# Slot 0's gather ahead of the last x_new stores, expert 1's loads held for slot 1's rows

## The reference

```python
x = x + tanh(g_xattn) * matmul(fake_quant(layernorm(x)), fake_quant(ctx))      # ctx (2, 1024, 1024), 8-bit steps
x = x + tanh(g_ffn) * moe(layernorm(x))
# moe: logits = y @ W_gate + b_gate; the two best of 8 experts per token;
#      mean over the two of relu(y @ W_e[expert] + b_e[expert]),  W_e (8, 1024, 1024)
```

## Time and profile before

| | us |
|---|---|
| median of 3 runs | 361.48 |
| lowest and highest | 359.96, 361.72 |
| the profiled execution | 358.4 |
| its span in the trace | 356.6 |
| TensorE busy (matmuls) | 311.2 |
| VectorE busy | 242.3 |
| GpSimd busy | 170.7 |
| ScalarE busy | 152.0 |

### The profile page before, as it was taken

How to read it: one execution, slowest core, us unless ns; L and a number is a source line. 1 busy time by engine, 2 the same in 40 slices (tenths; PEclk the granted TensorE clock), 3 DMA queues, 4 the chain that set the end, 5 groups by cost and what they waited for, 6 DMA issues and landing times.

```text
span 356.6 us, 6660 instructions
## 1 busy us (share of the span) xinstructions
PE 311.2 (87%) x1590; PEld 237.5 (67%) x1599; DVE 242.3 (68%) x328; ACT 152.0 (43%) x167; POOL 170.7 (48%) x168
## 2 busy tenths in 40 slices
PE   4488989999743999999999979999999999999920
PEld 1133336879712687888878868888888888888810
DVE  3789999998750897589975955985339854954520
ACT  3868979855352191076713610811118114600100
POOL 5647610000044473674845755746547465757430
PEclk9999999996585999999999989999999999999985
DMA  6999913335876569679999996896558965646432
GB/s 226 414 409 388 376 78 119 141 156 180 348 201 274 209 233 391 136 172 377 340 419 266 286 348 143 205 413 187 115 118 214 404 156 145 134 78 140 76 78 45
DMA packets 19965, 81.47 MB, mean 228 GB/s; under 512 B 4208, under 2 KB 4208, under 8 KB 15856
## 3 DMA queue, kind: packets, MB, share of 16 engines
q1 hardware_dynamic: 12272, 57.71, 42.5%
q0 software_dynamic: 7536, 23.60, 28.2%
q10 hardware_dynamic: 144, 0.01, 0.0%
HBM read 62.43 MB, written 18.87 MB: 228 GB/s over the span
## 4 chain that ended last, share of the span: by engine, by line
PE 49%; DVE 17%; DMA 13%; issue 8%; ACT 6%; DVEq 3%; POOL 1%; ACTq 1%; SPq 0%; POOLq 0%
PE ps L1254 37%; DMA out_dram<-res,sidx 6%; DVE w_lo L859 3%; PE ps_y L1078 2%; PE ps L1051 2%; DMA y_rows<-y_scratch,idx 2%; ACT w_hi L673 2%; DVE st L721 2%; DMA stage<-in_L_ffn_W_e_dram 2%; DMA stage<-in_ctx_dram 2%; PE ps_s L1103 2%; DVEq L287 2%; PE ps_q L1103 2%; DVE xt L777 1%; DVE res L1013 1%
## 5 line engine op out<-in xcount | busy, mean ns | idle before, releaser
L473 POOL DMA_INDIRECT y_rows<-y_scratch,gidx x88 | 107.2, 1218 | 35.0 <-issue 25.9
L1254 PE MATMUL ps<-w_hi,yT_hi 128*128 x320 | 99.6, 393 | 3.5 <-DVE yT_lo L853 3.5
L1254 PE MATMUL ps<-w_lo,yT_hi 128*128 x320 | 99.2, 391 | 0.0
L1254 PE MATMUL ps<-w_hi,yT_lo 128*128 x320 | 99.0, 391 | 0.0
L1254 PEld LDWEIGHTS ps<-w_hi,yT_hi 128*128 128x128 f32 x320 | 60.1, 189 | 17.6 <-issue 5.4
L859 DVE TENSOR_TENSOR w_lo<-stage,w_hi 128x2048 f32 (+1 forms) x32 | 71.2, 2278 | 0.9 <-ACT w_hi L673 0.8
L1254 PEld LDWEIGHTS ps<-w_lo,yT_hi 128*128 128x128 f32 x320 | 60.6, 189 | 12.6
L1254 PEld LDWEIGHTS ps<-w_hi,yT_lo 128*128 128x128 f32 x320 | 60.4, 189 | 12.7
L644 ACT ACTIVATE yT_hi<-ps_y 128x1024 fp32r<-128x1024 f32 x21 | 21.5, 1023 | 106.4 <-PE ps L1254 74.8
L499 POOL DMA_INDIRECT out_dram<-res,sidx x20 | 32.3, 1616 | 66.6 <-DVE res L1015 44.1
L1013 DVE TENSOR_TENSOR res<-ps,bias 128x1024 f32<-128x1024 f32 x20 | 24.4, 1220 | 47.6 <-PE ps L1254 37.4
(11 more groups left out here) (163 smaller groups left out, 248.8 us busy)
## 6 DMA issues: line engine op xcount, KB each, us to landing
stage<-in_L_ffn_W_e_dram SPq DMA_DIRECT2D x32, 1024.0 KB, 7.4
stage<-in_ctx_dram SPq DMA_DIRECT2D x16, 512.0 KB, 11.2
xt<-in_x_dram SPq DMA_DIRECT2D x8, 512.0 KB, 11.1
y_scratch<-y SPq DMA_DIRECT2D x8, 512.0 KB, 3.4
bias<-in_L_ffn_b_e_dram SPq DMA_DIRECT2D x8, 512.0 KB, 4.8
out_dram<-xt SPq DMA_DIRECT2D x6, 512.0 KB, 5.7
y_rows<-y_scratch,gidx POOLq DMA_INDIRECT x88, 4.4
out_dram<-xt POOLq DMA_DIRECT2D x2, 512.0 KB
```

The source lines that it names most:

```text
L473: pool.indirect_dma_start(out=y_rows[q][:, b * QD:(b + 1) * QD], out_offset=None, in_=y_quarters[:, :], in_offset=bass.IndirectOffsetOnAxi ...
L1254: last = pe.matmul(ps[q][:, h * 512:(h + 1) * 512], lhs[q][:, k, :], w[:, bass.ds(woff + k * D + h * 512, 512)], start=(k == 0 and lhs is ...
```

## The change

- POOL: three small indirect gathers of row 0 of W_gate into a new tile `prime` come after its last centring; the stores of x_new 6 and 7 move from ahead of slot 0's gather to behind slot 2's.
- SyncE: expert 1's chunks 0 and 1 go ahead of y stores 4 to 7. After x_new 0 to 3 the queue waits for slot 0's rows, then come bias 0 and x_new 4 and 5; it waits for slot 1's rows, then come bias 1 and chunks 2 and 3.
- ScalarE: the adds for tiles 6 and 7 come after the evacuation of slot 0; the waits for the x_new stores move from ahead of the slot loop to `sidx` (tiles 6 and 7) and to the splits (tiles 0 to 5).
- VectorE: the row sums of batch row 0 are read after the second slot matrix; the low split of chunk 2 goes ahead of slot 0's `yT_lo`; the waits for the stores move to the result's step.
- TensorE: the row-sum products and the place-rows products change places with the second count, and 18 clock-keeping matmuls stand in one place instead of 2 and 14.

```diff
--- before.py
+++ after.py
@@ -144,6 +144,7 @@
         idx = sb("idx", [P, E * SPE], u32)
         weight = sb("weight", [P, E * SPE], f32)
         qidx = sb("qidx", [P, (E + 1) * SPE, NQ], u32)
+        prime = sb("prime", [P, 3, E], f32)
         gidx = sb("gidx", [P, 2, NQ], u32)
         sidx = sb("sidx", [P, 2], u32)
 
@@ -230,6 +231,7 @@
         s_free = sem("slot_psum_free")
         s_post = sem("slot_result_ready")
         s_sc = sem("slot_scattered")
+        s_prime = sem("queue_primed")
         s_settled = sem("waits_settled")
 
         block = ctx.enter_context(nc.Block())
@@ -339,15 +341,19 @@
                 load_w0(c)
             for i in range(TPB):
                 store_y(i)
+            load_w1(0)
+            load_w1(1)
             for i in range(TPB, NT):
                 store_y(i)
-            load_w1(0)
-            load_w1(1)
-            for i in range(NT - 2):
+            for i in range(TPB):
                 store_x_new(i)
+            sp.wait_ge(s_g[0], 16)
             sp.wait_ge(s_qt, NT)
-            for e in range(2):
-                load_bias(e)
+            load_bias(0)
+            for i in range(TPB, NT - 2):
+                store_x_new(i)
+            sp.wait_ge(s_g[1], 16 * NQ)
+            load_bias(1)
             load_w1(2)
             load_w1(3)
             with sp.Fori(2, E) as n:
@@ -463,9 +469,10 @@
             pool.iota(iota_pe[:, :, :], [[1, P], [0, E]], base=0, channel_multiplier=0,
                       allow_small_or_imprecise_dtypes=True).then_inc(s_iota, 1)
             centre_q1(6)
-            for i in (NT - 2, NT - 1):
-                pool.wait_ge(s_oa, i + 1)
-                pool.dma_start(out_t[i], xt[:, i, :]).then_inc(s_sc, 16)
+            for j in range(3):
+                pool.indirect_dma_start(out=prime[:, j, :], out_offset=None, in_=W_gate[:, :],
+                                        in_offset=bass.IndirectOffsetOnAxis(ap=qidx[:, E * SPE, 0:1], axis=0)
+                                        ).then_inc(s_prime, 16)
 
             def gather(q):
 
@@ -484,8 +491,12 @@
             pool.wait_ge(s_gi, 2)
             pool.wait_ge(s_perm, 2)
             gather(0)
+            for i in (NT - 2, NT - 1):
+                pool.wait_ge(s_oa, i + 1)
+                pool.dma_start(out_t[i], xt[:, i, :]).then_inc(s_sc, 16)
             pool.wait_ge(s_oi, 16 * (NT - 2))
             pool.wait_ge(s_sc, 32)
+            pool.wait_ge(s_prime, 48)
 
             def step(slot, q, turn):
                 pool.wait_ge(s_gi, slot * 2 + 3)
@@ -636,7 +647,7 @@
             keep_yT(6)
             normalise(7)
             keep_yT(7)
-            for i in range(NT):
+            for i in range(NT - 2):
                 add_rowsum(i)
 
             def evacuate_hi(slot, q):
@@ -660,9 +671,9 @@
                                ACT.Copy).then_inc(s_perm, 1)
             act.wait_ge(s_tp, 1)
             evacuate_hi(0, 0)
+            for i in (NT - 2, NT - 1):
+                add_rowsum(i)
             act.wait_ge(s_tab, 1)
-            act.wait_ge(s_oi, 16 * (NT - 2))
-            act.wait_ge(s_sc, 32)
 
             def step(slot, q, turn):
                 act.wait_ge(s_mm, slot + 1)
@@ -677,11 +688,13 @@
                 act.wait_ge(s_tp, slot + 2)
                 evacuate_hi(slot + 1, 1 - q)
                 pick_rows(slot + 3, 1 - q)
+                act.wait_ge(s_sc, 32)
                 act.wait_ge(s_sc, slot * 16 + 16)
                 settle(act)
                 col = entry(act, COL, slot, E * SPE - 1)
                 act.activation(sidx[:, q:q + 1], idx[:, bass.ds(col, 1)], ACT.Copy).then_inc(s_gi, 1)
                 with act.If(nxt > 0):
+                    act.wait_ge(s_oi, 16 * (NT - 2))
                     for c in range(NCH):
                         split_hi(c)
                 act.nop()
@@ -919,11 +932,11 @@
             make_onehot(3)
             select(1)
             sign(1)
-            read_rowsums(0)
             positions(1)
             make_onehot(4)
             make_onehot(5)
             slot_matrix(1)
+            read_rowsums(0)
             select(2)
             make_onehot(6)
             sign(2)
@@ -982,14 +995,12 @@
                 dve.transpose(ps_y[:, :, :].rearrange("p k (b r) -> p k b r", b=NQ),
                               y_rows[q][:, :].rearrange("p (b k r) -> p k b r", b=NQ, k=KT)).then_inc(s_tp, 1)
 
+            split_lo(2, 3, slice(2 * CW, 3 * CW))
             dve.wait_ge(s_eh, 1)
             evacuate_lo(0)
-            for c in range(NCH // 2, NCH):
-                split_lo(c, c + 1, slice(c * CW, (c + 1) * CW))
+            split_lo(3, 4, slice(3 * CW, 4 * CW))
             dve.wait_ge(s_el, 1)
             turn_rows(1, 1)
-            dve.wait_ge(s_oi, 16 * (NT - 2))
-            dve.wait_ge(s_sc, 32)
 
             def step(slot, q, turn):
                 nxt = entry(dve, NXT, slot, E - 1)
@@ -1009,6 +1020,7 @@
                         settle(dve)
                 col = entry(dve, COL, slot, E * SPE - 1)
                 dve.wait_ge(s_mm, slot + 2)
+                dve.wait_ge(s_sc, 32)
                 dve.wait_ge(s_sc, slot * 16 + 16)
                 dve.tensor_tensor(res[q][:, :], ps[q][:, :], bias[:, bass.ds(woff >> 3, D)], ALU.add).then_inc(s_free, 1)
                 dve.wait_ge(s_free, slot + 3)
@@ -1213,22 +1225,20 @@
             pe.wait_ge(s_xn, NT - 1)
             pe.matmul(ps_i.rearrange("p (a b) -> p a b", b=E), ones_b[:, :],
                       sel[:, NT:NT + 1, :].to_broadcast([P, SPE, E]), start=True, stop=False)
-            place_rows(0, 0, 2)
             transpose_y(7)
+            counts(1)
             rowsums(0)
-            counts(1)
             gate(7)
-            place_rows(0, 2, TPB)
+            place_rows(0, 0, TPB)
             counts(2)
             place_rows(1, TPB, NT - 1)
             place_rows(2, NT - 1, NT)
-            keep_clock(2, ps[0][:, 512:1024])
             pe.wait_ge(s_abs, 1)
             for b in range(NQ):
                 last = pe.matmul(ps_r[:, b * E * SPE:(b + 1) * E * SPE], spread[:, b, :], tok_abs[:, :], start=True, stop=True)
             last.then_inc(s_spread, 1)
             rowsums(1)
-            keep_clock(14, ps[0][:, 512:1024])
+            keep_clock(18, ps[0][:, 512:1024])
             for k in range(KT):
                 if k % (KT // 2) == 0:
                     pe.wait_ge(s_perm, 1 + k // (KT // 2))
```

## The result

The changed kernel takes 364.35 us (median of 4 runs, 362.63 to 365.95) against 360.72 for the kernel before (4 runs, 358.06 to 361.72). The ratio is 1.0126, 95% interval 1.0073 to 1.018: slower by 0.7 to 1.8%. The forecast was 358.5, so it had the wrong sign. The profiled execution took 364.41 us, with a span of 362.6.

The account below looks back on a forecast made before the run. Taken as bound: the chain through expert 1's weight splitting and scatters, then TensorE from 208.82 us. Split 3.4 us earlier, 0.6 clock loss, a tenth or two for indices: -3.0, 361.5 to 358.5 us; range 353.7 to 361.8.

Parts of the forecast that it names:

- The frame: TensorE's earlier start at slot 0 pays only as far as the splitting of expert 1's weights comes earlier too.
- Slot 0's first matmul: TensorE's start on slot 0: at 106.5 us, 11.4 us earlier, with ends of 106.0 and 113.0.
- GpSimd's gathers: Eight quarter gathers for slots 1 and 2: 10.0 us, plus 2.0 for stretching under VectorE's splits, ending at 113.1.
- The failed step: Landing of the x_new 6 and 7 stores, ahead of expert 1's split: near 120.5, bounds 117.5 and 124.6.
- Rival 2: No change: stores count as landed only when the whole backlog has moved, 122.1 to 123.5; some 361.0 us; chance 0.21.
- Rival 3: Slower: backlog at 297 GB/s or less, stores last, landing 125.5; +2.2 us, 363.7 us; chance 0.10.
- From landing to split: On ScalarE, from the x_new stores' landing to expert 1's first split: 1.2 us.
- S: How much earlier ScalarE starts expert 1's first split: 3.4 us, at 121.7 instead of 125.14.
- The clock: Half clock on TensorE after the idle gap before slot 2: 2.0 us lost, 1.4 hidden behind scatter 1, loss 0.6.
- The sum: Whole kernel: -3.4 + 0.6 = -2.8, and a tenth or two for earlier indices: -3.0 us.
- The second slow stretch: Slow clock behind TensorE's gap ending at 208.82: may vanish for up to 2.0 us gain; none taken.
- Early loads, small gathers: Expert 1's chunks 0 and 1: cost 0, 1 us at most; GpSimd's small gathers: nothing, bounds 0.1 gain, 0.5 loss.

Follow-up runs that it names:

- the repeat: The kernel before, unchanged, profiled a second time: 360.98 us, span 359.2, indices at 100.57 us; ratio 0.9973.
- e10: The changed kernel without SyncE's hold for slot 0's rows, the hold for slot 1's rows kept: ratio 1.0132.
- e6: The changed kernel without SyncE's two holds, for slot 0's and slot 1's rows: ratio 0.9884.
- e9: The changed kernel without SyncE's hold for slot 1's rows, the hold for slot 0's rows kept: ratio 0.9987.
- e5: The kernel before with only slot 0's gather moved ahead of the stores of x_new 6 and 7: ratio 0.9815.
- e12: The changed kernel without the three small gathers on GpSimd and their wait: ratio 1.0149.
- e7: The changed kernel without both SyncE holds and with the stores of x_new 6 and 7 ahead of slot 2's gathers: ratio 0.987.
- e3: The changed kernel with the stores of x_new 6 and 7 between slot 1's and slot 2's gathers: ratio 1.0008.

## Why the prediction was wrong

Times of the forecast are moved by the 3.66 us that lie between the two traces of the kernel before, so that they compare with the repeat.

- **The frame was right.** "a PE start that is x us earlier is worth x only if the splitting of expert 1 comes x us earlier too": TensorE's start came 9.8 us earlier, and the whole of it was lost. From split to slot 2 it is 15.3 us before, in the repeat and after (125.14 to 140.42, 128.76 to 144.10, 130.20 to 145.47).
- **Slot 0's first matmul**: 11.4 us earlier forecast, 9.8 measured. ScalarE takes up the rows when it was to (105.25; 105.4 forecast); the missing 1.6 us lie between there and the first matmul, and cost nothing at the end. Indices: 0.35 and 0.7. Slot 1's pick: 104.7 forecast, 104.49 measured.
- **GpSimd's gathers**: two were lengthened, to 2.93 and 2.00, 3.0 us of stretch where 2.0 was forecast. First store 117.1 forecast, 117.69 measured.
- **The failed step: "The stores, sharing from 115.2, land near 120.5."** That is 6.0 us from the second issue; it took 10.67. In the repeat's frame it is 124.2 forecast and 129.0 measured: 4.8 us. Three things were wrong in it. The stores got no equal share, but landed behind the whole backlog; by the prediction's own sum that ends at 122.1, 125.8 in this frame, 1.6 later than 124.2. The backlog moved more slowly: 4.2 MB were to take 11.1 us from 111 (114.7 here), and took about 13.2 from 113.8 to 127, some 317 GB/s, 1.2 later. And between the end of the bulk and the landing lie 2.0 us more, for which the prediction had no term. Together 4.8; even its outer bound, 124.6, is 128.3 here. Behind it all stands a cause that no rival named: I had counted the volume, but not that the holds leave the queues at 111 and 114 GB/s from 100 to 108 and at 166 from 112 to 116, so that everything comes at once. Rival 2 had the first of the three: its backlog is moved at 123.5 at the latest, 127.2 here, which is what the windows show, but without the last 2 us. Rival 3 had the first two, "297 GB/s or less" and "the stores last", and a landing at 125.5, or 129.2 here, right to 0.2 us. I gave it 0.10. Part of that hit is luck: the rate until 127 was above 297, and the 2.0 us made up for it.
- **From landing to split**: 1.2 forecast, 1.2 measured. So S is -1.4 instead of 3.4.
- **The clock**: 2.0 us of loss forecast, "of that, 1.4 hide". Measured 2.55 (13.74 against 11.19), and 2.1 came through (86.3 against 84.2). The cover isn't a fixed amount: 1.4 us was hidden wholly in e10, 1.3 in e6, but of 2.5 in e9 only 1.0. The step missed by 1.5 us. Keeping the clock gave the loss back. The row from which the price was read doesn't show it: the 0.55 and 0.59 stand behind an idle gap of 1.79 us in the first trace, but the repeat has the same gap (1.95 us, at 212.94) and a clock of 1.00 behind it.
- **The sum**: -3.0 forecast, plus 4.8, plus 1.5, makes 3.3; the spans differ by 3.4.
- **The second slow stretch** at 208 is no term at all. The last block is 130.88 long in the repeat and 130.87 after; 132.51 occurred in the first trace, and 132.49 in e5, whose ratio is the best. As the kernel before has it in one execution and not in the other, it says nothing of the change.
- **Early loads, small gathers**: forecast at nothing. For the small gathers e12 bears that out within what the runs can tell. The early loads stay open: in the changed kernel's trace they share the stretch at 72 us with the y stores (329 GB/s against 144), and its indices still come 0.7 us ahead of the repeat's; but putting them back gave 1.0076 against 1.0126, and the indices of the kernels with them lie later on average.

The Trainium skill, "DMA: Bandwidth & Descriptors", section "Queues, rings and completion order", states two rules that pull apart here. By its round-robin between queues, packet by packet, two stores of 1.05 MB together that share half of some 350 GB/s would need about 6 us (an estimate from the windows), as I had taken. By its completion order the increment follows every earlier write of that engine on any queue. The tile views have the stores landing 10.67 us after issue, at 129.0, and the later of the chunks 12.2 after its issue at 114.7, at 126.9. This agrees with the second rule, by which the stores can't be counted before the chunks have landed, as do e6 and e7, whose stores land within a us of each other though issued 7 us apart. It doesn't prove it: unequal shares would look the same, no run tells the two apart, and the 2.1 us between 126.9 and 129.0 follow from neither.

Shown by runs: the wait for the stores, the weights in front of them as its cause, the hold that puts them there, and the clock. Open: the rule inside the DMA engines, and the last 2 us before the landing; what the early loads cost (about half a per cent, or nothing) and what the new order brings; and what sets the stretches of low clock that come and go.

## What to carry to other kernels

A transfer that is held until other data has arrived doesn't make room, it makes a crowd: the bytes come back later, in front of whatever is issued next, so before adding a hold, list what is issued in the few us behind its release and who waits for that. A small store issued behind megabytes on another queue landed here after those had moved; forecast it so, and not by its share. Moving such a store to the front is no cure while the crowd stands: in e3 slot 2's rows waited in its place. And take a second profile of the unchanged kernel before comparing stages: here two executions of it lay 3.7 us apart at 100 us, as much as the effect. The same second profile shows whether a slow stretch behind a gap comes with the gap.

## What the runs showed of the hardware that was not expected

- The granted clock differs between executions of one kernel for the same work: in the kernel before 1.00 or 0.57 at 72 to 76 us, and 0.55 or 1.00 behind the same gap of 1.8 to 1.95 us before the last block.
- Stores of 512 KB landed 2.6 to 3.3 us after issue in the repeat; after the change two landed 8.8 and 10.7 behind 2.6 MB on the other queue:

```profile
DMA to landing us min/median/max: 2.6/3.0/3.3
```

```profile
DMA to landing us min/median/max: 8.8/9.7/10.7
```

  (first the repeat's output tile between 100 and 124 us, then the x_new tile after the change, 112 to 131).
- Issuing a gather took 0.94 to 0.95 us in the changed kernel, and 2.00 and 2.93 for two that began under a low split of VectorE (106.03 to 108.32, 110.84 to 113.12). One that began 0.14 us ahead of the second split took 0.94.
- After an idle gap of 11.66 us TensorE was granted half its clock (0.50 at 144 to 148, the level of 1.2 GHz), and the 48 matmul groups took 2.55 us more; with matmuls through the gap the clock stayed at 1.00.
